# Moving two of VectorE's sums behind the last low part of the turned queries in a fused attention and expert kernel

## Chip, cores and metric

One core of a Trainium2 chip. The metric is the device time of one execution in microseconds, from before the first to after the last instruction; smaller is better. All times below are microseconds.

## What is computed

There are 32 batches of x, each 128 channels by 1024 positions, with a context of the same size. All is float32.

```python
x = x + xattn(layernorm(x), ctx, Wq, Wkv, Wout, b_out, g)
x = x + ffn(layernorm(x), A, B, Wr)

def xattn(x, context, Wq, Wkv, Wout, b_out, g):      # 8 heads of 64
    q = split_heads(einsum('oc,bcn->bon', Wq, x))
    k, v = map(split_heads, split(einsum('oc,bcn->bon', Wkv, context)))
    q = softmax(q, axis=-2) * 64 ** -0.5             # over the 64 values of a head
    k = softmax(k, axis=-1)                          # over the positions
    ctx = einsum('bhdn,bhen->bhde', k, v)
    out = einsum('bhde,bhdn->bhen', ctx, q)
    out = einsum('oc,bcn->bon', Wout, merge_heads(out)) + b_out
    return (out - mean(out)) * rsqrt(var(out) + 1e-5) * g
```

The ffn weighs 64 experts of rank 16 by a softmax over the 16 best scores of each row; it is the second stage of the kernel and the change doesn't touch it.

## The kernel before

The kernel has two stages. The first does the attention of all batches, the second the expert layer. Within each, every engine has its own instruction stream in an order written out by hand, and the engines meet only at semaphores. Nothing is reordered by the hardware or by a planner: an instruction that waits holds up all that stands behind it on its engine.

The first stage goes in passes, `step(s)`, from -1 to 33, each about one batch. A pass holds the keys and queries of batch s, the turning of keys and queries of batch s - 1 (`DELAY` 1) and the last output product of batch s - 2. Matrix products are made in three parts from a high and a low half of each operand (`split_products`, lines 52 to 54), so each operand on its way to TensorE gets a high part (a copy, mostly on ScalarE) and a low part (a subtraction, on VectorE or GpSimd).

The eight kinds of work of a pass that matter here:

- `queries` (TensorE, four chunks a pass), then on VectorE `max_queries` (L877) and `shift_queries` (L883), on ScalarE `exp_queries` (L630), on VectorE `sum_queries` (L889) and `invert_sums` (L894), and on GpSimd `norm_queries` (L513). `sum_queries` reads and writes SBUF only.
- `keys` (TensorE, four chunks), then `min_keys` (VectorE, L898) and `exp_keys` (ScalarE, L635).
- `turn_keys` (TensorE, L1256, four jobs KT0 to KT3): eight transposes each of the exponentials of the batch before.
- `turn_query` (TensorE, L1246, QT0 to QT3), then `query_hi` (ScalarE, L624) and `query_lo` (VectorE, L869): the high and the low part of the turned queries.
- `turn_context` (TensorE, L1264, C0), then `context_turned_hi` (ScalarE, L682) and `context_turned_lo` (VectorE, L934).
- `add_weighted` (TensorE): the weighted values from the turned keys, whose low part is GpSimd's `keys_lo` (L517).
- `fold` (TensorE, M0), then `folded_hi` (ScalarE, L660) and `folded_lo` (VectorE, L929).
- `add_output` (TensorE): the output product of the turned queries and the folded weights. ScalarE's `norm_x` (L665, L668, L671) and `x_hi` (L677) make the next batch's x.

TensorE writes into three pairs of PSUM banks in turn (a fourth is the accumulator). The order of the pairs is the ring

```python
RING = ["KT0", "Q0", "KT1", "K0", "KT2", "Q1", "KT3", "K1", "Q2",
        "QT0", "K2", "M0", "QT1", "Q3", "QT2", "K3", "QT3", "C0"]
SLOTS = 3
```

and `wait_slot` lets a job start when the job three places before it in the ring (of the pass before, where the ring begins anew) has been read by its last reader: for KT1 that is C0, read by `context_turned_lo`; for K3 it is QT1, read by `query_lo`; for KT0 it is K3, read by `exp_keys`.

TensorE's own order differs a little from the ring, as the accumulator's products stand between. From the fold on it is: `fold`, QT1, Q3, QT2, `add_output` 0, K3, `add_output` 1, QT3, C0, `add_output` 2, and in the next pass KT0, Q0, KT1, `add_output` 3, K0, KT2, Q1, `add_weighted` 0, KT3, `add_weighted` 1, K1, Q2, QT0, `add_weighted` 2 and 3, K2.

ScalarE's order in the second half of a pass: `exp_keys` 2, `folded_hi`, `query_hi` 1, `exp_queries` 2, `query_hi` 2, `norm_x`, `x_hi`, `query_hi` 3, `exp_keys` 3, `context_turned_hi`, `exp_queries` 3. GpSimd's at the end of a pass: `x_lo`, `norm_queries` 1 and 2, and in the next pass `keys_lo` 0 and 1, `norm_queries` 3, `keys_lo` 2 and 3.

`invert_sums(i)` waits for the sum of chunk i, and `norm_queries(i)` for its inverse.

Of the kernel before, what the change touches and what calls it, by code (L numbers as in the profile page):

```python
# [37 lines left out]
def wait_for(eng, sem, value):  # L38

    if isinstance(value, int) and value <= 0:  # L40
        return
    eng.wait_ge(sem, value)
# [48 lines left out]
def xattn_ffn(nc, x, context, Wq, Wkv, Wout, b_out, g, A, B, Wr, out):  # L91
# [4 lines left out]
    with ExitStack() as ctx:  # L96
# [141 lines left out]
        def on(kind, s, edge):  # L238

            return not edge or 0 <= s - DELAY[kind] < BATCHES  # L240
# [597 lines left out]
        def _(dve):  # L838
            def weights():


                dve.wait_ge(qk_turned, 1)
                dve.tensor_copy(wq_hi[:, :], wqT).then_inc(qk_hi_ready, 1)
                dve.tensor_scalar(wk_hi[:, :], wkT, -1.0, None, ALU.mult).then_inc(qk_hi_ready, 1)
                dve.wait_ge(qk_hi_ready, 2)
                dve.tensor_tensor(wq_lo[:, :], wqT, wq_hi[:, :].bitcast(F32), ALU.subtract).then_inc(qk_lo_ready, 1)
                dve.scalar_tensor_tensor(out=wk_lo[:, :], in0=wkT, scalar=-1.0, in1=wk_hi[:, :].bitcast(F32),
                                         op0=ALU.mult, op1=ALU.subtract).then_inc(qk_lo_ready, 1)

                dve.wait_ge(wo_turned, 1)  # L850
                woT3 = woT.rearrange("p (j c) -> p j c", j=CH)
                dve.reduce_sum(wo_sum[:, :], woT3, axis=X).then_inc(wo_step, 1)
                dve.reduce_sum(b_mean[:, :], b_rows, axis=X).then_inc(b_step, 1)
                dve.wait_ge(wo_step, 1)
                dve.tensor_scalar(wo_mean[:, :], wo_sum[:, :], 1.0 / P, None, ALU.mult).then_inc(wo_step, 1)
                dve.wait_ge(b_step, 1)
                dve.tensor_scalar(b_mean[:, :], b_mean[:, :], 1.0 / P, None, ALU.mult).then_inc(b_step, 1)
                dve.wait_ge(wo_step, 2)
                dve.wait_ge(pairs_zeroed, 1)
                for h in range(2):  # L860
                    r = slice(h * DH, (h + 1) * DH)
                    dve.tensor_tensor(wo_pairs[r, :, h, :], woT3[r, :, :], per_row(wo_mean[r, :], CH, P),
                                      ALU.subtract).then_inc(wo_centred, 1)
                dve.wait_ge(b_step, 2)
                dve.tensor_tensor(w["bias"][:, :], b_col[:, :], b_mean[:, :], ALU.subtract).then_inc(b_step, 1)
# [7 lines left out]
            def max_queries(b, i):  # L873

                dve.wait_ge(q_made, 4 * b + i + 1)
                src = flat(f"Q{i}").rearrange("p (g d) -> p g d", d=DH)
                dve.tensor_reduce(q_max[:, i, :], src, X, ALU.max).then_inc(q_max_ready, 1)  # L877
# [8 lines left out]
            def sum_queries(b, p, i):  # L886
                dve.wait_ge(q_exp, 4 * b + i + 1)
                v = eq[p][:, 2 * i:2 * i + 2, :].rearrange("p n (h d) -> p (n h) d", d=DH)
                dve.tensor_reduce(q_sum[:, i, :], v, X, ALU.add).then_inc(q_summed, 1)  # L889

            def invert_sums(b, i):
                dve.wait_ge(q_summed, 4 * b + i + 1)
                wait_for(dve, q_normed, 4 * b + i - 3)
                dve.reciprocal(q_inv[:, i, :], q_sum[:, i, :]).then_inc(q_inv_ready, 1)  # L894
# [48 lines left out]
            def average_matrix():  # L943
                dve.tensor_reduce(ident_sum[:, :], ident[:, :].rearrange("p (c j) -> p j c", j=BLK), X,
                                  ALU.add).then_inc(ident_summed, 1)
                dve.wait_ge(ident_summed, 1)
                dve.tensor_scalar(row_mean[:, :].rearrange("p (c j) -> p c j", j=BLK),
                                  ident_sum[:, :].unsqueeze(1).broadcast_to([P, QB, BLK]), 1.0 / P, None,
                                  ALU.mult).then_inc(row_mean_ready, 1)
# [132 lines left out]
            def last_step(par):  # L1082

                turn_back(0, 0)
                weight_lo(0)
                sum_queries(LAST, 1 - par, 3)
                invert_sums(LAST, 3)
                invert_keys(LAST, 1 - par)
                residual(0, 0, 0)
                weight_lo(1)  # L1090
                block_rows(1, 1)
                weight_lo(2)
                shift_rows(0)
                sum_squares(1)
                weight_lo(3)
                query_lo(LAST, 1 - par, 0)
                turn_rows(0)
                variance(1)
                weight_lo(4)
                weighted_lo(LAST)  # L1100
                weight_lo(5)
                folded_lo(LAST)
                query_lo(LAST, 1 - par, 1)
                weight_lo(6)
                query_lo(LAST, 1 - par, 2)
                weight_lo(7)
                turn_back(1, 1)
                query_lo(LAST, 1 - par, 3)
                weight_lo(8)
                block_rows(2, 0)  # L1110

            def step(s, par, edge):
                if edge and s == BATCHES:
                    last_step(par)
                    return
                X_, K, Q, C, KT, M, QT, O = (on(k, s, edge) for k in STAGES)
                if edge and s == LAST:
                    average_matrix()
                if edge and s == 0:
                    weights()  # L1120
                if edge and s == 1:
                    dve.wait_ge(z_hi_ready, 1)
                    dve.scalar_tensor_tensor(out=z_lo[:, :], in0=z_sum, scalar=DH ** -0.5, in1=z_hi[:, :].bitcast(F32),
                                             op0=ALU.mult, op1=ALU.subtract).then_inc(z_lo_ready, 1)
                if Q:
                    max_queries(s, 0)
                    shift_queries(s, par, 0)
                if K:
                    min_keys(s, par, 0)
                if KT:  # L1130
                    sum_queries(s - 1, 1 - par, 3)
                    invert_sums(s - 1, 3)
                if QT:
                    invert_keys(s - 1, 1 - par)
                if Q:
                    max_queries(s, 1)
                if X_:
                    stats_x(s + 1, 1 - par, 0)
                if Q:
                    shift_queries(s, par, 1)  # L1140
                if edge and s == LAST:
                    block_rows(0, 0)
                if X_:
                    stats_x(s + 1, 1 - par, 1)
                if Q:
                    sum_queries(s, par, 0)
                if K:
                    min_keys(s, par, 1)
                if edge and s == LAST:
                    sum_squares(0)  # L1150
                if Q:
                    max_queries(s, 2)
                if X_:
                    mean_x(s + 1)
                if edge and s == LAST:
                    variance(0)
                if Q:
                    shift_queries(s, par, 2)
                if QT:
                    query_lo(s - 1, 1 - par, 0)  # L1160
                if KT:
                    weighted_lo(s - 1)
                if K:
                    min_keys(s, par, 2)
                if Q:
                    invert_sums(s, 0)
                if M:
                    folded_lo(s - 1)
                if Q:
                    sum_queries(s, par, 1)  # L1170
                if QT:
                    query_lo(s - 1, 1 - par, 1)
                if Q:
                    max_queries(s, 3)
                    shift_queries(s, par, 3)
                if QT:
                    query_lo(s - 1, 1 - par, 2)
                if K:
                    min_keys(s, par, 3)
                if Q:  # L1180
                    sum_queries(s, par, 2)
                if QT:
                    query_lo(s - 1, 1 - par, 3)
                if Q:
                    invert_sums(s, 1)
                if C:
                    context_turned_lo(s)
                if Q:
                    invert_sums(s, 2)

            each_step(dve, step)
            each_mix(dve, mix_step)

# [293 lines left out]
```

## Time and profile before

| | |
|---|---|
| median of 3 runs | 1889.69 (1888.95 to 1889.94) |
| the profiled execution | 1887.64, its span from first to last instruction 1885.9 |
| TensorE, matmuls | busy 1812.2 (96%) |
| TensorE, weight loads | busy 1559.3 (83%) |
| VectorE | busy 1494.7 (79%) |
| ScalarE | busy 1044.4 (55%) |
| GpSimd | busy 1138.7 (60%) |
| mean granted TensorE clock | 0.99 |

The span goes from the first to the last recorded instruction. Busy times are sums over the whole span and say nothing of which engine another waits for. Matmuls are pipelined, so the distance between the starts of two is what counts, not the duration of one. In an order of time the number in brackets is how long the engine was idle before a row, and the arrow names what ended that idle time.

### The profile page before, as it was taken

The page shows a single profiled execution, that of the slowest core. Times are in us where ns is not written, and L with a number is a line of the kernel's source. Part 1 is how long each engine was busy: PE and PEld are TensorE (multiplying, and loading weights), DVE is VectorE, ACT ScalarE, POOL GpSimd, SP SyncE. Part 2 cuts the span into 40 slices and gives each one's busy share as a digit, 9 for nine tenths or more (in the row PEclk, how much of TensorE's full clock was granted, in tenths as well). Part 3 has the DMA queues.
Part 4 walks back from the last instruction along what each step waited for, and adds up shares of the span by engine and source line. Part 5 has one row for each costly group of instructions (what it writes and reads, how often), then busy time and mean ns, then how long its engine had stood idle before and what let it go on. Part 6 is the DMA issues. An engine that isn't in the chain of part 4 may idle for free.

```text
span 1885.9 us, 28175 instructions
## 1 busy us (share of the span) xinstructions
PE 1812.2 (96%) x9820; PEld 1559.3 (83%) x9820; DVE 1494.7 (79%) x1983; ACT 1044.4 (55%) x1267; POOL 1138.7 (60%) x552
## 2 busy tenths in 40 slices
PE   5999999999999999999999987999999999999998
PEld 4788788788878878888887776999999999999997
DVE  6988888888888888888888976777777777777751
ACT  3878787887878788787878753222222222222210
POOL 3757666675766667576666744555555555555541
PEclk9999999999999999999999988999999999999999
DMA  4112122221212222121222353444444444444431
GB/s 129 49 59 84 59 73 68 70 60 58 83 58 72 70 70 61 58 83 58 72 70 89 105 187 107 165 164 157 156 156 156 157 159 162 158 162 163 163 128 62
DMA packets 156651, 199.12 MB, mean 106 GB/s; under 512 B 75904, under 2 KB 118528, under 8 KB 156608
## 3 DMA queue, kind: packets, MB, share of 16 engines
q1 hardware_dynamic: 142960, 174.95, 28.5%
q0 software_dynamic: 4608, 16.78, 2.9%
q10 hardware_dynamic: 9040, 6.82, 1.2%
q8 instruction: 26, 0.43, 0.1%
q14 instruction: 17, 0.14, 0.0%
HBM read 131.40 MB, written 71.30 MB: 107 GB/s over the span
## 4 chain that ended last, share of the span: by engine, by line
PE 77%; DVE 9%; issue 8%; ACT 5%; DMA 0%; SPq 0%; ACTq 0%; POOL 0%; POOLq 0%; DVEq 0%
PE ps L52 23%; PE ps L54 22%; PE ps L53 22%; PE ps L1256 6%; PE ps L1246 3%; DVE k_min L898 2%; ACT ek L635 2%; DVE ql L869 2%; DVE m_lo L929 1%; DVE q_sum L889 1%; ACT m_hi L660 1%; ACT qh L624 1%; ACT xn L671 1%; DVE w_b_lo L940 1%; DMA g<-in_L_xattn_g 0%
## 5 line engine op out<-in xcount | busy, mean ns | idle before, releaser
L513 POOL TENSOR_TENSOR eq<-eq,q_inv 128x1024 f32<-128x1024 f32 x128 | 242.5, 1904 | 132.7 <-DVE q_inv L894 132.7
L517 POOL TENSOR_TENSOR kT_lo<-kT,kT_hi 128x1024 fp32r<-128x1024 f32 x128 | 304.5, 2401 | 1.5 <-ACT kT_hi L617 1.4
L538 POOL TENSOR_TENSOR xT_lo<-work,xT_hi 128x1024 fp32r<-128x1024 f32 x32 | 76.5, 2392 | 312.7 <-ACT xT_hi L709 312.7
L52 PE MATMUL ps<-w_ra_hi,xT_hi 128*128 128x384 f32 (+1 forms) x768 | 251.1, 327 | 0.0
L54 PE MATMUL ps<-w_ra_hi,xT_lo 128*128 128x384 f32 (+1 forms) x768 | 251.0, 327 | 0.0
L53 PE MATMUL ps<-w_ra_lo,xT_hi 128*128 128x384 f32 (+1 forms) x768 | 251.0, 327 | 0.0
L635 ACT ACTIVATE ek<-ps,k_min 128x1024 f32<-128x1024 f32 x128 | 142.3, 1112 | 118.7 <-DVE k_min L898 118.7
L52 PE MATMUL ps<-w_b_hi,hT_hi 128*128 128x512 f32 x512 | 203.4, 397 | 3.6 <-POOL hT_lo L543 3.6
L54 PE MATMUL ps<-w_b_hi,hT_lo 128*128 128x512 f32 x512 | 201.3, 393 | 0.0
L53 PE MATMUL ps<-w_b_lo,hT_hi 128*128 128x512 f32 x512 | 200.8, 392 | 0.0
L528 POOL TENSOR_TENSOR rstd_c<-var_c,minus_half 128x32 f32<-128x32 f32 x32 | 174.4, 5451 | 25.1 <-DVE var_c L964 25.1
L898 DVE TENSOR_REDUCE k_min<-ps 128x1 f32<-128x1024 f32 x128 | 156.4, 1222 | 36.4 <-PE ps L54 34.6
L507 POOL TENSOR_TENSOR xn_lo<-xn,xn_hi 128x1024 fp32r<-128x1024 f32 x32 | 76.6, 2392 | 165.9 <-ACT xn_hi L677 165.9
L877 DVE TENSOR_REDUCE q_max<-ps 128x16 f32<-128x1024 f32 x128 | 156.0, 1219 | 18.9 <-PE ps L54 14.7
L624 ACT ACTIVATE qh<-ps,k_inv 128x1024 fp32r<-128x1024 f32 x128 | 142.7, 1115 | 48.5 <-PE ps L54 44.3
L869 DVE SCALAR_TENSOR_TENSOR ql<-ps,k_inv,qh 128x1024 fp32r<-128x1024 f32 x128 | 163.5, 1277 | 3.0 <-ACT qh L624 2.0
L883 DVE TENSOR_TENSOR eq<-ps,q_max 128x1024 f32<-128x1024 f32 x128 | 155.9, 1218 | 2.2
L889 DVE TENSOR_REDUCE q_sum<-eq 128x16 f32<-128x1024 f32 x128 | 154.8, 1209 | 1.0
L698 ACT ACTIVATE ps<-o_blk 128x1024 f32<-128x1024 f32 x29 | 29.8, 1029 | 215.5 <-DVE o_blk L954 215.5
L52 PEld LDWEIGHTS ps<-w_ra_hi,xT_hi 128*128 128x128 f32 x768 | 145.0, 189 | 1.2
L53 PEld LDWEIGHTS ps<-w_ra_lo,xT_hi 128*128 128x128 f32 x768 | 144.9, 189 | 1.2
L1256 PEld LDWEIGHTS ps<-ident,ek 128*128 128x128 f32 x1024 | 116.7, 140 | 34.3 <-ACT ek L635 17.3
(142 smaller groups left out, 4798.0 us busy)
## 6 DMA issues: line engine op xcount, KB each, us to landing
x_sb<-in_x SPq DMA_DIRECT2D x64, 512.0 KB, 4.4
ctx_hi<-in_ctx POOLq DMA_DIRECT2D x32, 512.0 KB, 3.7
ctx_sb<-in_ctx SPq DMA_DIRECT2D x32, 512.0 KB, 3.4
attention_out<-o_sb SPq DMA_DIRECT2D x32, 512.0 KB, 2.6
o_sb<-attention_out SPq DMA_DIRECT2D x32, 512.0 KB, 4.7
x_turn<-x_blk SPq DMA_DIRECT2D x32, 512.0 KB, 2.6
work<-x_turn SPq DMA_DIRECT2D x128, 128.0 KB, 2.8
h_turn<-h_blk SPq DMA_DIRECT2D x32, 512.0 KB, 3.4
```

What stands on the lines that cost most here:

```text
L52: pe.matmul(out, stat_hi, mov_hi, start=first, stop=False)
L53: pe.matmul(out, stat_hi, mov_lo, start=False, stop=False)
L54: return pe.matmul(out, stat_lo, mov_hi, start=False, stop=last)
L513: pool.tensor_tensor(v, v, per_row(q_inv[:, i, :], 2 * HEADS, DH), ALU.mult).then_inc(q_normed, 1)
L517: pool.tensor_tensor(kT_lo[:, i % 2, :, :], kT[:, i % 2, :, :], kT_hi[:, i % 2, :, :].bitcast(F32), ALU.subtract).then_inc(kT_lo_ready, 1)
L528: pool.tensor_tensor(rstd_c[:, :], var_c[:, :], w["minus_half"][:, 0:1].broadcast_to([P, NBLK]), ALU.pow).then_inc(rstd_c_ready, 1)
L624: act.activation(q_hi[:, j % 2, :], flat(f"QT{j}"), ACT.Copy, bias=0.0, scale=k_inv[:, p, j:j + 1]).then_inc(q_hi_ready, 1)
L635: act.activation(ek[p][:, i, :], flat(f"K{i}"), ACT.Exp, bias=k_min[:, p, i:i + 1], scale=-1.0, accum_out=k_sum[:, p, i:i + 1]).then_inc(k ...
L869: dve.scalar_tensor_tensor(out=q_lo[:, j % 2, :], in0=flat(f"QT{j}"), scalar=k_inv[:, p, j:j + 1], in1=q_hi[:, j % 2, :].bitcast(F32), op0 ...
L889: dve.tensor_reduce(q_sum[:, i, :], v, X, ALU.add).then_inc(q_summed, 1)
L898: dve.tensor_reduce(k_min[:, p, i:i + 1], flat(f"K{i}"), X, ALU.min).then_inc(k_min_ready, 1)
L1256: last = pe.transpose(out[:, n, j * P:(j + 1) * P], ek[1 - par][:, j, c:c + P], ident[:, :])
```

## The change

In VectorE's `step`, `sum_queries` for chunks 1 and 2 is taken from its two places (chunk 1 ahead of `query_lo` 1, chunk 2 ahead of `query_lo` 3) and put behind `query_lo` 3, ahead of `invert_sums` 1. The number of instructions, their operands and the semaphores stay as they are, and the other engines' streams aren't touched.

```diff
                 if M:
                     folded_lo(s - 1)
-                if Q:
-                    sum_queries(s, par, 1)
                 if QT:
                     query_lo(s - 1, 1 - par, 1)
                 if Q:
@@
                     query_lo(s - 1, 1 - par, 2)
                 if K:
                     min_keys(s, par, 3)
-                if Q:
-                    sum_queries(s, par, 2)
                 if QT:
                     query_lo(s - 1, 1 - par, 3)
                 if Q:
+                    sum_queries(s, par, 1)
+                    sum_queries(s, par, 2)
                     invert_sums(s, 1)
                 if C:
                     context_turned_lo(s)
```

## Rows read from the trace of the kernel before

**Rows 1.** The page: busy time, share of the span, instructions of TensorE.

```profile
PE 1812.2 (96%) x9820; PEld 1559.3 (83%) x9820; DVE 1494.7 (79%) x1983; ACT 1044.4 (55%) x1267; POOL 1138.7 (60%) x552
```

**Rows 2.** Stretches: busy time of each engine in one pass, clock, DMA.

```profile
605.25:638.28 33.03, 32.40 (x180) 26.70 (x181) 29.27 (x34) 26.74 (x34) 22.85 (x13) 1.00 0.24 68
```

**Rows 3.** Order of time, TensorE: start, length, line, operands, idle before.

```profile
622.06 0.39 PE L52 MATMUL ps<-kT_hi,cT_hi 128*128 128x512 f32 x1
...
631.50 0.40 PE L54 MATMUL ps<-qh,m_lo 128*128 128x512 f32 x1
631.98 0.49 PE L52 MATMUL ps<-ctx_hi,wk_hi 128*128 128x512 f32 x1
...
637.74 0.39 PE L54 MATMUL ps<-qh,m_lo 128*128 128x512 f32 x1
638.28 1.06 PE L1256 MATMUL ps<-ident,ek 128*128 128x128 f32 x8 [0.15 <-ACT ek L635]
639.10 0.48 PE L52 MATMUL ps<-wq_hi,xn_hi 128*128 128x512 f32 x1
...
640.58 1.04 PE L1256 MATMUL ps<-ident,ek 128*128 128x128 f32 x8
641.37 0.47 PE L52 MATMUL ps<-qh,m_hi 128*128 128x512 f32 x1
```

**Rows 4.** Order of time, VectorE, the same pass.

```profile
612.53 1.21 DVE L889 TENSOR_REDUCE q_sum<-eq 128x16 f32<-128x1024 f32 x1
613.78 0.25 DVE L894 RECIPROCAL q_inv<-q_sum 128x16 f32<-128x16 f32 x1
...
627.95 1.41 DVE L929 TENSOR_TENSOR m_lo<-ps,m_hi 64x512 fp32r<-64x512 f32 x2 [1.58 <-ACT m_hi L660]
629.38 1.22 DVE L889 TENSOR_REDUCE q_sum<-eq 128x16 f32<-128x1024 f32 x1
630.64 1.28 DVE L869 SCALAR_TENSOR_TENSOR ql<-ps,k_inv,qh 128x1024 fp32r<-128x1024 f32 x1
...
635.42 1.22 DVE L898 TENSOR_REDUCE k_min<-ps 128x1 f32<-128x1024 f32 x1
636.55 1.21 DVE L889 TENSOR_REDUCE q_sum<-eq 128x16 f32<-128x1024 f32 x1
637.68 1.27 DVE L869 SCALAR_TENSOR_TENSOR ql<-ps,k_inv,qh 128x1024 fp32r<-128x1024 f32 x1
638.87 0.24 DVE L894 RECIPROCAL q_inv<-q_sum 128x16 f32<-128x16 f32 x1
639.07 1.22 DVE L934 TENSOR_TENSOR cT_lo<-ps,cT_hi 128x1024 fp32r<-128x1024 f32 x1
```

**Rows 5.** Order of time, ScalarE, the same pass: high parts 1, 2 and 3.

```profile
628.55 1.11 ACT L624 ACTIVATE qh<-ps,k_inv 128x1024 fp32r<-128x1024 f32 x1
...
631.99 1.12 ACT L624 ACTIVATE qh<-ps,k_inv 128x1024 fp32r<-128x1024 f32 x1 [1.38 <-PE ps L54]
...
635.93 1.11 ACT L624 ACTIVATE qh<-ps,k_inv 128x1024 fp32r<-128x1024 f32 x1
```

**Rows 6.** Order of time in the pass after the last queries, several engines.

```profile
1070.34 1.09 PE L1256 MATMUL ps<-ident,ek 128*128 128x128 f32 x8 [0.37 <-DVE cT_lo L934]
...
1092.52 1.91 PE L1246 MATMUL ps<-ident,eq 128*128 128x128 f32 x8
...
1098.05 1.12 ACT L624 ACTIVATE qh<-ps,k_inv 128x1024 fp32r<-128x1024 f32 x1 [1.30 <-PE ps L54]
...
1099.20 1.28 DVE L869 SCALAR_TENSOR_TENSOR ql<-ps,k_inv,qh 128x1024 fp32r<-128x1024 f32 x1 [1.17 <-ACT qh L624]
```

**Rows 7.** Order of time, GpSimd: norms of queries 1 and 2, last key low parts.

```profile
639.19 3.77 POOL L513 TENSOR_TENSOR eq<-eq,q_inv 128x1024 f32<-128x1024 f32 x2 [0.63 <-DVE q_inv L894]
...
649.51 4.75 POOL L517 TENSOR_TENSOR kT_lo<-kT,kT_hi 128x1024 fp32r<-128x1024 f32 x2
```

**Rows 8.** Stretches at the end of the first stage, columns as in rows 2.

```profile
1076.00:1083.00 7.00, 4.63 (x31) 3.79 (x30) 6.83 (x9) 4.92 (x7) 6.82 (x4) 1.00 0.67 264
```

## The prediction

> **What bounds the kernel now.** I read the page first: TensorE has a matmul in flight for 96% of the span [rows 1]. Then the table by stretches over one pass of the first stage: a pass is 33.03 us, TensorE is busy for 32.40 of it at a granted clock of 1.00, and VectorE for 29.27 [rows 2]. The first stage repeats that pass once for each batch, so what the change does to one pass is multiplied by about 31. TensorE's order of time shows how small its pauses are. Unhindered, 512-column matmuls start 0.23 apart; before the fourth key product they start 0.48 apart (631.50 to 631.98), and before the first turn of the keys 0.54 (637.74 to 638.28) [rows 3]. These two pauses, 0.25 and 0.31, are near the path that the change touches.
>
> The third view is VectorE's order of time [rows 4]. From 629.38 to 640.4 it has no idle time: sum 1, low part 1, maxima and shift of query chunk 3, low part 2, key minimum 3, sum 2, low part 3, inverse 1, low part of the turned context, inverse 2. (Chunks are numbered from 0, as in the code: sums 1 and 2 are those of the second and third query chunks, low part 3 that of the last turned queries.) The fourth is ScalarE's [rows 5]: high part 3 runs from 635.93 to 637.04, and low part 3 can't start before it. Now low part 3 starts at 637.68, after sum 2. So between 635.42 + 1.13 = 636.55 (key minimum 3 lets go of VectorE) and 637.04, VectorE would have nothing else to do: sum 2 fills time in which the next instruction isn't ready. This is the fact on which the forecast turns.
>
> **Part 1: sum 1 leaves its place before low part 1.** High part 1 ends at 628.55 + 1.11 = 629.66 [rows 5]. A low part that waits for its high part starts 0.03 behind it: 1098.05 + 1.12 = 1099.17, and 1099.20 [rows 6]. So low part 1 starts at 629.69, not 630.64, 0.95 earlier; VectorE idles for 0.33 behind the folded weights, which end at 627.95 + 1.41 = 629.36 [rows 4]. The fourth key product waits for low part 1 (630.64 + 1.28 = 631.92, and 631.98: a release takes 0.06 from VectorE to TensorE) [rows 3, 4]. Its pause of 0.25 goes, since low part 1 now ends at 630.97, before 631.73. But the gain has nowhere to go: the next pause, at 638.28, is a wait for the key exponential of ScalarE, and ScalarE's queue ahead of it (high part 2 at 631.99, the norm of x, high part 3) starts when the first output product ends, at about 631.9 [rows 3, 5]. That product stands ahead of the fourth key product and isn't earlier. So TensorE reaches its next wait 0.25 sooner and leaves it at the same 638.28. Value taken: nothing; the other bound is 0.25 a pass, if some of it comes through.
>
> **Part 2: sum 2 leaves its place before low part 3.** Everything from low part 1 on is 0.95 earlier, so VectorE is free for low part 3 at 636.55 - 0.95 = 635.60. High part 3 still ends at 635.93 + 1.11 = 637.04, so low part 3 starts at 637.07 and 1.47 is spent idle. It is 0.61 earlier than before. Who waits for it is the first query product, which begins at 639.10 right behind the transposes and gains nothing [rows 3].
>
> **Part 3: both sums now stand ahead of the turned context.** Steps between starts are from VectorE's rows [rows 4]: a low part 1.19 (637.68 to 638.87), a sum 1.13 (636.55 to 637.68), inverse 1 to the turned context's low part 0.20 (638.87 to 639.07), and this 1.22 long. The new end of the turned context's low part is 637.07 + 1.19 + 1.13 + 1.13 + 0.20 + 1.22 = 641.94, where it was 639.07 + 1.22 = 640.29. Its reader is TensorE's second turn of the keys, whose PSUM pair it frees (C0 and KT1 share one). That turn starts at 640.58 with nothing idle before it, so the room is 0.29 less 0.06. In the pass after the last queries TensorE is already seen idle at this very place for this very producer, 0.37 [rows 6]. With the release it starts at 642.00, 1.42 later. Eight transposes behind a pause take 0.82 (638.28 to 639.10), without one 0.79 (640.58 to 641.37) [rows 3]: 0.03 more. Sum: 1.45 a pass.
>
> Does the pass take this back? TensorE is in order, so all behind the turn moves by 1.45: key products, weighted values, fold, turned queries, first output product, and with this ScalarE's queue and high part 3. That closes a ring: high part 3, low part 3, two sums, turned context, second turn of the keys, TensorE's work up to the first output product, high parts and norm of x, high part 3 again. Nothing in it waits for the clock of another engine with slack, so the pass is 33.03 + 1.45 = 34.48. GpSimd follows: the norms of queries 1 and 2 begin 0.08 behind inverse 1 (638.87 + 0.24 = 639.11, and 639.19) [rows 4, 7]. Inverse 1 stood 1.71 ahead of the second turn of the keys and will stand at 640.52, 1.48 ahead, so GpSimd is 0.23 later against TensorE. Its last key low part ends at 649.51 + 4.75 = 654.26, and its reader comes at 622.06 + 33.03 = 655.09 [rows 3, 7]: 0.83 of room, so it costs nothing; without that room it would cost the 0.23.
>
> No instruction, byte or DMA is added. Low parts 1 to 3 and the turned context's occur in 31 passes with both neighbours (batches 1 to 31 with the turned queries of the one before). In the first pass there are no turned queries and the order alone changes little. 31 x 1.45 = 45.0. On the profiled execution's 1887.64 that is 1932.6; the median of the runs, 1889.69, stands 2.05 above it, so the forecast is 1889.69 + 45.0 = **1934.7 us**.
>
> Bounds: if a sum followed by an inverse costs as in 612.53 to 613.78, 1.25 and not 1.13, the pass costs 1.57 and the whole 48.7 [rows 4]. If the 0.25 of part 1 comes through after all, it is 1.20 and 37.2. The first pass and the handover to the second stage, where VectorE's order is closed too, I bound by a little under two passes' worth, 2.5, either way.
>
> **What two rules would make of it.** TensorE's weight loads are busy for 26.70 of the 33.03 [rows 2], 81%, while matmuls are in flight for 98%. The Trainium skill (Perfetto Trace Analysis, Identifying the Most-Contended Engine) says that matmul busy time misleads and that the weight loads' share tells the headroom. By that rule VectorE, 89% busy, is the fuller engine, TensorE could take 1.45 out of 6.33 and the result would be no change, 1889.7. The trace speaks against it at this place: the matmuls ahead of the turn start 0.23 apart without a hole. I weigh it as rival B.
>
> **Rivals.** A, *the order pays*: if high part 3 ended by 635.57, low part 3 would start at 635.60, the turned context's low part would end at 640.47 and its reader start at 640.53, on time. Then both pauses, 0.25 and 0.31, could go: 0.56 x 31 = 17.4 faster, 1872.3. The point that decides is 1.47 us of ScalarE, which the rows give only if the norm of x moved. Chance 0.04.
>
> B, *absorbed*: TensorE has the headroom or one of its other pauses shrinks by what this one grows, 1889.7. Against it: the ring above has no pause in it that isn't a latency. Chance 0.03, and 0.05 for an absorption of a half, 1912.
>
> C, *the clock*: a pause of 1.4 each pass lowers TensorE's clock. For it: eight transposes took 1.91 at the lower level (1.2 GHz) and 1.04 at the higher (2.4 GHz) [rows 3, 6]. Against it: around 1079 TensorE was busy for only 4.63 of 7.00, and 1.00 was granted [rows 8]. Were two us of each pass's matmuls at the lower level, some 1 us more each would make 31 and 1966. The Trainium skill (TensorE: Matmul & The Clock Gate, A second HAM failure mode: psum-queue depth-cycling) says that short, frequent pauses between groups of matmuls can make the clock swing; by it this rival would be the likelier, and no stretch of the first stage so far shows it. Chance 0.04.
>
> D, *GpSimd late*: its 0.23 isn't hidden by the 0.83, and adds 7 to 1942. Chance 0.04.
>
> **How the numbers follow.** The forecast has 0.80, and its own range is 1926 to 1941 (37.2 less one pass's worth, to 48.7 plus 2.5). A and B lie outside below, C above, a part of D inside; together they leave out less than 0.2, so this is the range. Faster by over 0.2% (about what a measurement of this kernel can tell from no change): A, 0.04. Within it: B, 0.03. Slower: the rest, 0.93.
>
> **What would show it.** The time between two second turns of the keys is 34.4 to 34.6. TensorE is idle for some 1.4 ahead of that turn, released by the turned context's low part, and no longer idle ahead of the fourth key product. VectorE idles for 0.33 ahead of low part 1 and about 1.5 ahead of low part 3, both released by ScalarE's high part. The clock stays at 1.00 in the stage. The forecast is wrong if high part 3 comes earlier, if the second turn of the keys starts without a pause, or if the second stage changes its length by more than 3 us.

## The result and the profile after

The changed kernel takes 1930.53 us (median of 5 runs, 1926.05 to 1931.18), the kernel before 1889.37 (5 runs, 1888.95 to 1889.94). The ratio is 1.0219, 95% interval 1.0208 to 1.0230: 41.2 slower. The forecast was 1934.7, with a range of 1926 to 1941.

TensorE's order of time around the turn of two passes, in the changed kernel. L1244, L1254 and L1262 are L1246, L1256 and L1264 of before [rows 3]; VectorE's line numbers that matter (L869, L889, L894, L934) are the same.

```profile
656.45 0.39 PE L54 MATMUL ps<-qh,m_lo 128*128 128x512 f32 x1
656.68 0.39 PE L52 MATMUL ps<-ctx_hi,wk_hi 128*128 128x512 f32 x1
...
662.30 0.39 PE L54 MATMUL ps<-qh,m_lo 128*128 128x512 f32 x1
663.22 1.06 PE L1254 MATMUL ps<-ident,ek 128*128 128x128 f32 x8 [0.54 <-ACT ek L635]
...
665.28 0.40 PE L54 MATMUL ps<-wq_hi,xn_lo 128*128 128x512 f32 x1
666.85 1.09 PE L1254 MATMUL ps<-ident,ek 128*128 128x128 f32 x8 [1.18 <-DVE cT_lo L934]
667.70 0.48 PE L52 MATMUL ps<-qh,m_hi 128*128 128x512 f32 x1
```

Three places are to be seen. Ahead of the fourth key product the starts are 0.23 apart: the pause of before is gone. Ahead of the first turn of the keys they are 0.92 apart, where they were 0.54: that pause took over what the other gave up. And ahead of the second turn of the keys they are 1.57 apart where they were 0.23 (640.35 in the row below, and 640.58 [rows 3]): the new pause, 1.34, ended by VectorE's low part of the turned context, as forecast. In the kernel before:

```profile
640.35 0.40 PE L54 MATMUL ps<-wq_hi,xn_lo 128*128 128x512 f32 x1
```

VectorE's order of time in the same pass [rows 4]:

```profile
652.89 1.41 DVE L929 TENSOR_TENSOR m_lo<-ps,m_hi 64x512 fp32r<-64x512 f32 x2 [1.58 <-ACT m_hi L660]
654.64 1.28 DVE L869 SCALAR_TENSOR_TENSOR ql<-ps,k_inv,qh 128x1024 fp32r<-128x1024 f32 x1 [0.34 <-ACT qh L624]
...
659.42 1.21 DVE L898 TENSOR_REDUCE k_min<-ps 128x1 f32<-128x1024 f32 x1
662.02 1.28 DVE L869 SCALAR_TENSOR_TENSOR ql<-ps,k_inv,qh 128x1024 fp32r<-128x1024 f32 x1 [1.38 <-ACT qh L624]
663.22 2.33 DVE L889 TENSOR_REDUCE q_sum<-eq 128x16 f32<-128x1024 f32 x2
665.47 0.24 DVE L894 RECIPROCAL q_inv<-q_sum 128x16 f32<-128x16 f32 x1
665.63 1.16 DVE L934 TENSOR_TENSOR cT_lo<-ps,cT_hi 128x1024 fp32r<-128x1024 f32 x1
```

The two gaps that the prediction named are there, 0.34 ahead of low part 1 and 1.38 ahead of low part 3, both ended by ScalarE's high parts. The second is where sum 2 used to be.

The chain that ended last, over the same stretch, walks the ring of the prediction piece by piece (start, length, what):

```profile
656.94 0.05 ACT qh L624
...
658.64 1.25 ACT xn L671
...
660.87 1.12 ACT qh L624
661.99 0.03 issue
662.02 1.28 DVE ql L869
663.30 1.13 DVE q_sum L889
```

Stretches, one pass of the changed kernel, columns as in [rows 2]:

```profile
628.82:663.22 34.40, 32.30 (x180) 26.73 (x181) 29.01 (x34) 26.89 (x34) 22.88 (x13) 1.00 0.22 66
```

The work is that of before, the pass is longer, and the granted clock is still 1.00. (This pass is one of the longer ones: they take 34.40 and 34.32 in turn.) To compare passes over the whole stage I take the turned context's low part, 32 times, once a pass (line, operation, count, shortest/median/longest ns, first and last start). First before, then after:

```profile
L934 DVE TENSOR_TENSOR cT_lo<-ps,cT_hi x32: 1224/1225/1226, 44.2 to 1069.1; 128x1024 fp32r<-128x1024 f32 x32
```

```profile
L934 DVE TENSOR_TENSOR cT_lo<-ps,cT_hi x32: 1159/1161/1165, 46.7 to 1112.6; 128x1024 fp32r<-128x1024 f32 x32
```

Between first and last lie 31 passes: 1024.9 before and 1065.9 after, 33.06 and 34.38 a pass, 1.32 more, 41.0 in all. (First and last pass are longer than the rest: those in the middle take 33.02 before and 34.36 on average after.) The first of the 32 starts 2.5 later, and behind the start of the last one 816.8 before and 816.7 after are left of the spans of 1885.9 and 1929.3. So the 43.4 by which the span of the profiled execution is longer are 41.0 from the passes, 2.5 from ahead of them, and nothing from the second stage.

### The profile page after: what moved, and what is told of

The parts are those of the page before. It is cut to its first block, busy times and chain, and to the rows that moved or that the text cites. A ratio compares the mean times of both kernels' runs of the same rounds, so it can differ in the third digit from the quotient of the medians.

```text
span 1929.3 us, 28175 instructions
## 1 busy us (share of the span) xinstructions
PE 1811.0 (94%) x9820; PEld 1560.4 (81%) x9820; DVE 1488.5 (77%) x1983; ACT 1048.8 (54%) x1267; POOL 1137.8 (59%) x552
## 4 chain that ended last, share of the span: by engine, by line
PE 70%; DVE 12%; issue 9%; ACT 7%; DMA 0%; POOL 0%; SPq 0%; ACTq 0%; POOLq 0%; DVEq 0%
PE ps L52 21%; PE ps L54 21%; PE ps L53 20%; PE ps L1254 4%; PE ps L1244 3%; DVE k_min L898 2%; ACT qh L624 2%; DVE q_sum L889 2%; ACT xn L671 2%; DVE cT_lo L934 2%; DVE ql L869 2%; DVE m_lo L929 1%; ACT m_hi L660 1%; ACT ek L635 1%; DVE w_b_lo L940 1%
## 5 line engine op out<-in xcount | busy, mean ns | idle before, releaser
L869 DVE SCALAR_TENSOR_TENSOR ql<-ps,k_inv,qh 128x1024 fp32r<-128x1024 f32 x128 | 163.7, 1279 | 53.1 <-ACT qh L624 53.1
L1254 PE MATMUL ps<-ident,ek 128*128 128x128 f32 x1024 | 135.6, 275 | 54.0 <-DVE cT_lo L934 37.1
L1254 PEld LDWEIGHTS ps<-ident,ek 128*128 128x128 f32 x1024 | 114.4, 140 | 88.8 <-DVE cT_lo L934 50.3
L889 DVE TENSOR_REDUCE q_sum<-eq 128x16 f32<-128x1024 f32 x128 | 151.8, 1207 | 0.0
L612 ACT COPY kT<-ps 128x1024 f32<-128x1024 f32 x128 | 129.7, 1014 | 33.2 <-PE ps L1254 33.2
```

Source lines behind the costliest of these rows:

```text
L869: dve.scalar_tensor_tensor(out=q_lo[:, j % 2, :], in0=flat(f"QT{j}"), scalar=k_inv[:, p, j:j + 1], in1=q_hi[:, j % 2, :].bitcast(F32), op0 ...
L1254: last = pe.transpose(out[:, n, j * P:(j + 1) * P], ek[1 - par][:, j, c:c + P], ident[:, :])
```

## The experiments

"A pass" below is always last start less first start of the turned context's low part, divided by 31, from each run's own profile; 33.06 is that of the kernel before. The kernels of one group ran on one chip with runs of the kernel before, whose medians there were 1888.28 (first four), 1887.94 (next four) and 1888.48 (last two).

| run | median | ratio to before, 95% interval | a pass |
|---|---|---|---|
| only sum 1 late | 1902.71 | 1.0055 to 1.0089 | 33.45 |
| only sum 2 late | 1896.77 | 1.0035 to 1.0068 | 33.31 |
| changed, sums 1 and 2 an eighth long | 1885.94 | 0.9984 to 1.0003 | 33.00 |
| before, sums 1 and 2 an eighth long | 1887.35 | 0.9986 to 1.0005 | 33.02 |
| changed, turned context ahead of the sums | 1981.34 | 1.0482 to 1.0514 | 35.99 |
| changed, norm of x early | 1917.61 | 1.0138 to 1.0169 | 34.04 |
| before, sum 1 in a gap | 1887.99 | 0.9992 to 1.0010 | 33.02 |
| sum 1 in a gap, norm of x early | 1877.55 | 0.9932 to 0.9959 | 32.70 |
| before, norm of x early | 1887.90 | 0.9989 to 1.0007 | 33.05 |
| changed, sums 1 and 2 half as long | 1896.12 | 1.0027 to 1.0058 | 33.32 |

**One sum at a time.** Against the kernel before, only sum 1 moved (inverse 1 then waits for the third sum, since sum 2 comes first):

```diff
-                dve.wait_ge(q_summed, 4 * b + i + 1)
+                dve.wait_ge(q_summed, 4 * b + (3 if i == 1 else i + 1))
@@
-                if Q:
-                    sum_queries(s, par, 1)
                 if QT:
                     query_lo(s - 1, 1 - par, 1)
@@
                 if Q:
+                    sum_queries(s, par, 1)
                     invert_sums(s, 1)
```

> Only sum 1 is moved behind low part 3; sum 2 keeps its old place ahead of it (inverse 1 waits for the third sum of its batch, as the sums now end in another order). Theory (the ring through the turned context): sum 2 fills VectorE's gap, low part 3 starts 0.03 behind high part 3 at 637.07 on the scale of the pass before, and from there to the second turn of the keys it was 4.83 in the trace of the changed kernel; one sum less is 3.70, and 0.11 for an inverse right behind its own sum, 3.81: 640.88, which is 0.30 late, with 0.03 for the transposes 0.33 a pass, 10 us in all, about 1900. Rival (each moved sum costs its own length): half of the whole loss, about 1910.

And only sum 2:

```diff
-                if Q:
-                    sum_queries(s, par, 2)
                 if QT:
                     query_lo(s - 1, 1 - par, 3)
                 if Q:
+                    sum_queries(s, par, 2)
                     invert_sums(s, 1)
```

> Only sum 2 is moved behind low part 3. Theory (ring): low part 3 still starts at 637.07, as the gap is now empty, and the second turn of the keys comes 3.70 behind it, at 640.77: 0.19 late, with the transposes 0.22 a pass, 7 us, about 1896. The pause ahead of the fourth key product stays. Rival (each moved sum costs its own length): about 1910. Rival (only the sum that leaves the gap matters, since the gap is what is lost): all of the loss, about 1930.

Together the parts cost 14.4 + 8.5 = 22.9, a good half of the 41.2 of both. That is the mark of slack with an edge: each moved sum first uses up the 0.61 by which low part 3 comes forward and the 0.23 of room (0.29 less 0.06) at the second turn of the keys, and two moved sums have both only once. That makes 0.84 a pass; the passes show 1.32 - 0.39 - 0.25 = 0.68. VectorE's rows of the run with sum 1 late:

```profile
609.34 1.21 DVE L889 TENSOR_REDUCE q_sum<-eq 128x16 f32<-128x1024 f32 x1
610.72 1.28 DVE L869 SCALAR_TENSOR_TENSOR ql<-ps,k_inv,qh 128x1024 fp32r<-128x1024 f32 x1 [0.17 <-ACT qh L624]
611.92 1.21 DVE L889 TENSOR_REDUCE q_sum<-eq 128x16 f32<-128x1024 f32 x1
613.25 0.25 DVE L894 RECIPROCAL q_inv<-q_sum 128x16 f32<-128x16 f32 x1
```

Sum 2 fills the gap ahead of low part 3 down to 0.17. The inverse follows its own sum by 1.33, more than the 1.24 that I had expected, so from low part 3 to the second turn of the keys (614.64) it is 3.92 and not 3.81. This 0.11 more than covers the 0.06 a pass by which the loss is larger than expected (0.39, expected 0.33). Both runs fit the ring. The rival by which each moved sum costs its own length (1910 for both) falls with both, and so does the one by which sum 2 alone is the whole loss.

**The length of the sums.** Added to the changed kernel, and to the kernel before; 56 of the 64 values of each head are left out of sums 1 and 2:

```diff
                 v = eq[p][:, 2 * i:2 * i + 2, :].rearrange("p n (h d) -> p (n h) d", d=DH)
+                if i in (1, 2):
+                    v = v[:, :, 0:8]
                 dve.tensor_reduce(q_sum[:, i, :], v, X, ALU.add).then_inc(q_summed, 1)
```

> The changed kernel with sums 1 and 2 over only 8 of the 64 values of each head (that part of the sum is left out), so that each takes VectorE some 0.3 and not 1.2. Theory (ring): the second turn of the keys is ready at about 640.2 and is on time at 640.58; the pass is 33.0 again, about 1889. If the pause that goes ahead of the fourth key product did reach the pass, 32.8 and about 1882. Rival (the order of the waits costs, not the length of the sums): stays at 1930.

> The kernel before with the same shortened sums 1 and 2 (the rest of the two sums is left out), in their old places. Theory: the ring of the kernel before runs through ScalarE's norm of x and its high part 3 and holds no sum, so 1.8 us less VectorE work a pass gives nothing: 33.0 a pass, about 1889; the pause ahead of the fourth key product goes and the next one grows by it. Rival (VectorE's load bounds the pass): up to 1.8 x 31 = 56 less, 1833, or 0.25 a pass and 1882 if that pause counts.

The changed order with short sums is as fast as the kernel before. So the order itself, with its waits, costs nothing that can be measured; the VectorE time between low part 3 and the turned context costs all. And the kernel before gains nothing within the interval from 1.8 us less VectorE work a pass: it wasn't bound by VectorE. TensorE's pauses with the changed order and short sums:

```profile
603.97 1.06 PE L1256 MATMUL ps<-ident,ek 128*128 128x128 f32 x8 [0.46 <-ACT ek L635]
...
628.11 1.09 PE L1246 MATMUL ps<-ident,eq 128*128 128x128 f32 x8 [0.26 <-DVE m_lo L931]
...
636.98 1.06 PE L1256 MATMUL ps<-ident,ek 128*128 128x128 f32 x8 [0.54 <-ACT ek L635]
```

The pause ahead of the second turn of the keys is gone, and the one ahead of the first stands at 0.46 and 0.54 where it was 0.15 [rows 3].

With `0:32` in place of `0:8` the sums are half as long, which asks for a slope:

> The changed kernel with sums 1 and 2 over 32 of the 64 values of each head (the other half of these sums is left out). Theory: each is 0.53 shorter, so the turned context's low part ends 1.07 sooner than in the changed kernel; the pass falls from 34.36 to 33.29, which is still above the 33.03 at which ScalarE's ring takes over: 33 less, about 1897. Rival (a threshold in the order, not a length): 1930 or 1889.

1896.12 against about 1897, and 33.32 a pass. Three lengths of the same two instructions in the same order, 1.2, 0.67 and 0.27 for one, give 34.38, 33.32 and 33.00: the first step is VectorE's time one for one (1.06 for the 1.07 forecast), and the second ends at the pass of before.

**The turned context first.** In the changed kernel:

```diff
-                if Q:
-                    sum_queries(s, par, 1)
-                    sum_queries(s, par, 2)
-                    invert_sums(s, 1)
                 if C:
                     context_turned_lo(s)
                 if Q:
+                    sum_queries(s, par, 1)
+                    sum_queries(s, par, 2)
+                    invert_sums(s, 1)
                     invert_sums(s, 2)
```

> The changed kernel with the turned context's low part taken ahead of the two sums: low part 3, turned context, sums 1 and 2, inverses 1 and 2. Theory: the second turn of the keys is on time again (its VectorE work ends at 640.29 on the scale of the pass before), but inverse 1 comes 3.5 later than before, so GpSimd norms queries 1 and 2 later and its key low parts come later still; against 0.83 of room that makes about 2.7 a pass, 84 in all, about 1970, with TensorE's pause now ahead of the weighted values and none ahead of the second turn of the keys. Rival (the context's wait is the only cost, the rest is hidden): about 1889. Rival (shift 0 late for the third turn of the keys, 1.2 a pass, and GpSimd hidden): about 1927.

1981.34, 2.93 a pass more than before, where 2.7 was expected. TensorE's pauses, and the two rows of GpSimd between them:

```profile
654.32 1.07 PE L1253 MATMUL ps<-ident,ek 128*128 128x128 f32 x8 [0.45 <-ACT ek L635]
...
661.75 1.09 PE L1253 MATMUL ps<-ident,ek 128*128 128x128 f32 x8 [1.35 <-DVE eq L883]
...
665.00 0.50 PE L52 MATMUL ps<-kT_hi,cT_hi 128*128 128x512 f32 x1 [0.76 <-POOL kT_lo L517]
```

```profile
658.83 3.77 POOL L513 TENSOR_TENSOR eq<-eq,q_inv 128x1024 f32<-128x1024 f32 x2 [4.22 <-DVE q_inv L894]
662.55 4.74 POOL L517 TENSOR_TENSOR kT_lo<-kT,kT_hi 128x1024 fp32r<-128x1024 f32 x2
```

There is none ahead of the second turn of the keys, which settles that its wait is a wait for the order on VectorE. TensorE's idle time is split: 1.35 for the shift of queries 0, ahead of the third turn, and 0.76 for GpSimd's key low part, behind it. The cause isn't split in this way. GpSimd starts its norms when VectorE's inverse 1 is there and goes from them to the key low parts without idle time, so the first of these ends at the same time whatever the third turn waits for, and it is the last wait: the one for the shift is spent inside it. The chain that ended last goes through GpSimd here too, and not through the shift. The expected place was right, and the rival by which the shift is late and GpSimd hidden (1927) falls.

**ScalarE's part of the ring.** The norm of the next x moves into two idle times of ScalarE, here in the changed kernel:

```diff
+                if X_:
+                    norm_x(s + 1, 1 - par)
                 if K:
                     exp_keys(s, par, 2)
@@
                 if Q:
                     exp_queries(s, par, 2)
+                if X_:
+                    x_hi(s + 1, 1 - par)
                 if QT:
                     query_hi(s - 1, 1 - par, 2)
-                if X_:
-                    norm_x(s + 1, 1 - par)
-                    x_hi(s + 1, 1 - par)
```

> The changed kernel with ScalarE's norm of the next x moved ahead of key exponential 2 and its high part behind query exponential 2, both into idle time of ScalarE, so that high part 3 waits for its transposes alone. Theory (high part 3 is a link of the ring, its start set by ScalarE's queue): it starts 0.39 sooner (in the trace of the changed kernel the transposes end at 660.45, it starts at 660.87), and the pass falls from 34.36 to 33.97: 12 less, about 1918. Rival A of the prediction (ScalarE 1.47 sooner, all of the loss gone): about 1889. Rival (ScalarE's queue is not in the ring): stays at 1930.

1917.61 and 34.04 a pass. ScalarE now waits for the transposes ahead of high part 3, and VectorE's idle time ahead of low part 3 is 0.99, down from 1.38:

```profile
652.88 1.12 ACT L624 ACTIVATE qh<-ps,k_inv 128x1024 fp32r<-128x1024 f32 x1 [2.42 <-PE ps L1245]
```

```profile
654.03 1.28 DVE L870 SCALAR_TENSOR_TENSOR ql<-ps,k_inv,qh 128x1024 fp32r<-128x1024 f32 x1 [0.99 <-ACT qh L624]
```

So the start of high part 3 is a link of the ring, and 0.39 on it are worth 0.34 a pass. The passes in the middle now take 34.00 each, and no longer 34.40 and 34.32 in turn. What rival A of the prediction asked for, 1.47 on this link, ScalarE can't give: its transposes are the next thing to hold it.

**Part 1 alone, and both links.** Against the kernel before, sum 1 goes the other way, ahead of the folded weights' low part:

```diff
+                if Q:
+                    sum_queries(s, par, 1)
                 if M:
                     folded_lo(s - 1)
-                if Q:
-                    sum_queries(s, par, 1)
                 if QT:
                     query_lo(s - 1, 1 - par, 1)
```

> The kernel before with sum 1 moved the other way, ahead of the folded weights' low part, where VectorE idles for 1.58 a pass; sum 2 stays. Low part 1 is then 0.95 earlier as in the change, and nothing stands behind low part 3. Theory: the pause of 0.25 ahead of the fourth key product goes, the one ahead of the first turn of the keys grows by as much, the pass stays 33.03: about 1889. Rival: the 0.25 comes through, 8 less, about 1881.

The same with ScalarE's norm of x early:

> Sum 1 ahead of the folded weights' low part as in the run before it, and ScalarE's norm of x early. Theory: with both links loosened high part 3 waits only for its transposes, which end 0.25 earlier; key exponential 3 and the first turn of the keys follow 0.25 to 0.28 earlier; the pass is about 32.76, 8 less than before: about 1881. Rival (something else closes the ring at 33.03): about 1889.

And the norm of x early alone, in the kernel before:

> The kernel before with ScalarE's norm of x early, both sums in their old places. Theory: in the kernel before two links meet within 0.05, ScalarE's queue (high part 3 at 635.93) and the transposes it reads (ready at 635.9, held back by the pause ahead of the fourth key product); loosening one of them gives nothing: 33.0 a pass, about 1888, while both together gave 1877.6. Rival (the norm alone made that gain): about 1878.

These make a square. Sum 1 in the gap alone 1887.99, the norm alone 1887.90, neither 1887.94 and 1888.48, both 1877.55: a ratio of 0.9945, interval 0.9932 to 0.9959, which beats both kernels. In the kernel before, high part 3 had two things to wait for that ended within 0.1 of each other, ScalarE's own queue and the transposes that it reads, and only taking away both moves it. With the norm early alone, ScalarE is idle ahead of high part 3 and the pass is as long as before (the transposes and high part 3 in that run, then the transposes in the kernel before):

```profile
635.77 1.04 PE L1247 MATMUL ps<-ident,eq 128*128 128x128 f32 x8
636.85 1.11 ACT L624 ACTIVATE qh<-ps,k_inv 128x1024 fp32r<-128x1024 f32 x1 [2.80 <-PE ps L1247]
```

```profile
634.85 1.03 PE L1246 MATMUL ps<-ident,eq 128*128 128x128 f32 x8
```

High part 3 starts 1.08 behind its transposes, and it was 1.08 in the kernel before too (634.85, and 635.93 [rows 5]). These transposes are held back by the pause ahead of the fourth key product, which is a wait for low part 1, behind sum 1. So the kernel before has a second ring of about the same length, and that one does go through VectorE.

That the gap for sum 1 is there and is filled is seen on VectorE, in the run with sum 1 alone (the idle time ahead of the folded weights was 1.58):

```profile
625.57 1.16 DVE L889 TENSOR_REDUCE q_sum<-eq 128x16 f32<-128x1024 f32 x1
627.23 1.41 DVE L929 TENSOR_TENSOR m_lo<-ps,m_hi 64x512 fp32r<-64x512 f32 x2 [0.50 <-ACT m_hi L660]
```

I had expected 8 from both together and 10.4 were measured. The pause ahead of the fourth key product, 0.25 in starts, costs a further 0.10, since behind it the next matmul follows at 0.33 (631.98 to 632.31), as behind the pause at 665.00 above (665.33), and not at 0.23.

## Why the prediction was right

**What bounds the kernel.** Right, and not complete. The kernel before is held by a ring through TensorE and ScalarE, not by VectorE's load: 1.8 us less of VectorE a pass gave 0.04. The prediction did not see that the transposes of high part 3 hold it just as long as ScalarE's queue does. That changes nothing in the forecast, since in the changed kernel the pause that holds them back is gone. Rows of a low part that waits for a high part, not shares of busy time, told which way the change goes.

**Part 1.** Right. The pause ahead of the fourth key product went, and none of it reached the pass while ScalarE's norm of x stood where it was (sum 1 in a gap, 33.02 against 33.06; 32.93 and 33.02 in turn in the middle, against 33.02).

**Part 2.** Right: 1.47 idle ahead of low part 3 forecast, 1.38 and 1.31 recorded in alternate passes.

**Part 3.** Right in its mechanism, 0.13 too large in its sum: 1.45 a pass forecast, 1.32 measured. From low part 3 to the second turn of the keys I had 4.87 + 0.06 = 4.93, and the trace has 666.85 - 662.02 = 4.83. The two sums were right (2.25 from the first to the inverse, forecast 2.26). The step from the inverse to the turned context's low part was not VectorE's own: in the kernel before ScalarE had just ended the high part,

```profile
638.03 1.01 ACT L682 CAST cT_hi<-ps 128x1024 fp32r<-128x1024 f32 x1
```

at 639.04, and the low part started 0.03 later, 0.20 behind the inverse [rows 4]. Where it is late anyway, that step is 0.16, and the instruction itself 1.16 and not 1.22. The term that was mis-sized is "inverse 1 to the turned context's low part 0.20, and this 1.22 long", together 1.42, measured 1.32. The rest is about half an alternation. Passes in which ScalarE's normalisation starts 0.40 behind its shift take 34.40 and those in which it starts 0.33 behind take 34.32, in turn like the two bodies of the loop:

```profile
658.24 0.29 ACT L668 ACTIVATE shift<-rstd,neg_mean 128x1 f32<-128x1 f32 x1
658.64 1.24 ACT L671 ACTIVATE xn<-x_sb,shift,rstd 128x1024 f32<-128x1024 f32 x1
...
692.64 0.29 ACT L668 ACTIVATE shift<-rstd,neg_mean 128x1 f32<-128x1 f32 x1
692.97 1.24 ACT L671 ACTIVATE xn<-x_sb,shift,rstd 128x1024 f32<-128x1024 f32 x1
```

The same step alternates in the kernel before (0.33 and 0.41), where the pass does not: there high part 3 waits for its transposes in the shorter case. It alternates with the norm early too, where the pass is 34.00 each time. So it reaches the pass only where ScalarE's queue is what holds high part 3. Why the step differs wasn't tested.

**The sum.** The 31 passes together are 41.0 longer; the medians differ by 41.2.

**The bounds.** The step of 1.25 from a sum to its inverse didn't come up, since the other sum stands between. It did with sum 1 late, as 1.33.

**The rivals.** A, the order pays: no. Its condition was tested as far as ScalarE allows, 0.39 of 1.47, and it gave back 13, in proportion. B, absorbed: no. TensorE's weight loads were busy 26.73 of 34.40, a still smaller share than before, and the loss went through whole. The Trainium skill (Perfetto Trace Analysis, Identifying the Most-Contended Engine) judges TensorE's headroom by that share. By this trace the share tells how full the engine is, not who waits for whom. C, the clock: no. 1.00 was granted in the pass and over 50 to 1112 as a whole, with a pause of 1.34 in each pass. The Trainium skill (TensorE: Matmul & The Clock Gate, A second HAM failure mode: psum-queue depth-cycling) says that frequent short pauses between groups of matmuls can make the clock swing; at this length the trace doesn't agree. D, GpSimd late: its norms of queries 1 and 2 start 1.06 ahead of the second turn of the keys (665.79, and 666.85) and not 1.39, 0.33 later and not 0.23, and nothing waits for it:

```profile
665.79 3.77 POOL L513 TENSOR_TENSOR eq<-eq,q_inv 128x1024 f32<-128x1024 f32 x2 [2.30 <-DVE q_inv L894]
669.52 4.76 POOL L517 TENSOR_TENSOR kT_lo<-kT,kT_hi 128x1024 fp32r<-128x1024 f32 x2
```

GpSimd became the last wait only when the inverses came after the turned context.

## What to carry to other kernels

In an order written by hand, look at what a cheap instruction stands in front of, and whether the next one would be ready: sum 2 looked like an obstacle ahead of a low part and was the filling of a wait. Moving it behind the wait spends its time twice, once idle and once ahead of a PSUM pair that TensorE needs next. Where a pass is a ring of waits, count one instruction's length against the room of its first reader, and ask of each link what else would hold it: two loosened links gave 10.4 here, each alone nothing. And where an engine pauses twice in a row, the idle times don't say how the loss is shared out: only the last wait counts.

## What was not expected of the hardware

The first pass of the profiled execution was 2.5 later at its turned context. Of this 2.3 are already there at the key minimum just ahead of the sums (40.85 before, 43.13 after), so the order explains about 0.2. In stretches, from 30 to 40 us, the kernel before and then the changed one:

```profile
30.00:40.00 10.00, 5.51 (x17) 4.08 (x18) 7.24 (x10) 6.97 (x10) 5.42 (x5) 0.85 0.18 52
```

```profile
30.00:40.00 10.00, 5.36 (x13) 3.67 (x13) 4.91 (x7) 5.61 (x9) 4.49 (x4) 0.50 0.17 52
```

TensorE's granted clock was 2.4 GHz for most of the stretch in the kernel before and 1.2 GHz throughout in the changed one, and 13 matmuls were done in place of 17. In both, TensorE had been idle for 2 to 3 at a time. The prediction's "no stretch of the first stage so far shows it" overlooks this one. The order is not the cause by itself: with the same order and short sums the clock of that stretch was 0.83, and over all ten experiments it was 0.66 to 0.88, with the low part's first start at 43.9 to 45.3. The fastest of the five runs of the changed kernel, 1926.05, has a mean clock of 0.990, the others 0.986 to 0.988. That the start of the kernel, where TensorE is busy for little more than half of the time, makes such differences between runs is likely from this; no run tested it.
